# A graph network of four layers on one core: the fourth edge stage without a loop on the engines

## The reference, cut to what matters

```python
x_dst = tfn_features[edge_dst]                  # gathered, one row of 64 for each edge
wk = relu(edge_features @ k_w1 + k_b1) @ k_w2 + k_b2
wv = relu(edge_features @ v_w1 + v_b1) @ v_w2 + v_b2
k = tensor_product(x_dst, edge_sh, wk, Cqk)     # w * sum over 9 harmonics of sh_s * (x @ C_s)
v = tensor_product(x_dst, edge_sh, wv, Cv)
attn = einsum('ehd,ehd->eh', q[edge_src], k)    # 8 heads of 16
ex = exp(attn - segment_max(attn)[edge_src])
alpha = ex / (segment_sum(ex)[edge_src] + 1e-16)
upd = segment_sum(v * alpha, edge_src) @ W_out
out = tfn_features @ W_self + upd               # then a batch norm over the nodes
```

## Time and profile before

| | |
|---|---|
| Median of 3 runs | 3519.25 us (3516.62 to 3521.51) |
| The profiled execution's own time | 3510.65 us |
| Its span, first to last instruction | 3508.9 us |
| Fourth edge stage in it, first product to last addition | about 2151 to 3445 us |
| Mean granted TensorE clock over the span | 0.805 |

### The profile page before, as it was taken

The page is one execution under the profiler, slowest core; times in us unless marked ns, Lnnn a source line. Parts: engine busy times, 40 slices in busy tenths (PEclk is TensorE's granted clock), DMA queues, the critical chain, the costliest instruction groups (busy, mean ns, idle before and its releaser), DMA issues. The chain is left out here.

```text
span 3508.9 us, 58176 instructions
## 1 busy us (share of the span) xinstructions
PE 2551.3 (73%) x14132; PEld 2166.8 (62%) x14132; DVE 2280.8 (65%) x5044; ACT 1062.1 (30%) x2723; POOL 1789.0 (51%) x1813
## 2 busy tenths in 40 slices
PE   3778777514554444357777765999999999999986
PEld 2778776413443333245555544888888888888872
DVE  3555555337887887855556542677777777777775
ACT  1111111134554564111111101344444344443441
POOL 2777776066666663157777723444444344443400
PEclk7776777556555666589999967999999999999985
DMA  2443443265554552035445517988888888888830
GB/s 64 93 87 84 87 87 64 46 161 131 132 123 125 132 124 72 2 110 157 153 153 161 158 63 177 203 204 197 197 201 199 200 198 190 193 200 198 195 92 9
DMA packets 433884, 475.50 MB, mean 136 GB/s; under 512 B 200837, under 2 KB 304648, under 8 KB 433712
## 3 DMA queue, kind: packets, MB, share of 16 engines
q1 hardware_dynamic: 358832, 295.60, 35.9%
q0 software_dynamic: 59904, 123.64, 15.2%
q10 hardware_dynamic: 14976, 54.53, 4.5%
HBM read 408.18 MB, written 65.34 MB: 135 GB/s over the span
## 5 line engine op out<-in xcount | busy, mean ns | idle before, releaser
L1960 PE MATMUL psum<-ckv,z 128*128 128x256 f32 x4160 | 969.7, 384 | 0.0
L1960 PEld LDWEIGHTS psum<-ckv,z 128*128 128x128 f32 x4160 | 767.9, 191 | 98.5
L1823 POOL DMA_INDIRECT ga<-XX,src_i x416 | 398.1, 957 | 449.7 <-PE psum L1941 307.0
L985 POOL DMA_INDIRECT ga<-T,src_i x416 | 431.4, 1037 | 302.3 <-issue 112.5
L275 POOL DMA_INDIRECT ga<-T,src_i x416 | 401.3, 965 | 151.7 <-issue 124.4
L275 POOL DMA_INDIRECT ga<-TA,src_i x416 | 412.4, 991 | 126.7 <-issue 126.7
L2009 DVE TENSOR_TENSOR z<-psum,shb 128x2560 f32<-128x2560 f32 x104 | 293.7, 2824 | 125.8 <-PE psum L1941 78.5
L455 PE MATMUL psum<-wre,re 128*128 128x68 f32 x832 | 213.4, 349 | 142.1 <-DVE oneT L331 82.6
L1816 POOL TENSOR_TENSOR acc<-acc,wkv 128x512 f32<-128x512 f32 x104 | 114.3, 1099 | 332.7 <-DMA wkv<-WKV 316.4
L455 PEld LDWEIGHTS psum<-wre,re 128*128 128x128 f32 x832 | 173.4, 258 | 162.9 <-issue 153.9
L2050 DVE TENSOR_TENSOR acc<-acc,psum 128x256 f32 x416 | 175.4, 422 | 120.2 <-PE psum L1932 90.9
(11 more groups left out here) (349 smaller groups left out, 4862.8 us busy)
## 6 DMA issues: line engine op xcount, KB each, us to landing
shb<-in_ea SPq DMA_DIRECT2D x104, 640.0 KB
WKV<-wkvo ACTq DMA_DIRECT2D x104, 512.0 KB
shb<-in_ea SPq DMA_DIRECT2D x104, 512.0 KB
wkv<-WKV SPq DMA_DIRECT2D x104, 512.0 KB
dl<-DL SPq DMA_DIRECT2D x312, 128.0 KB, 3.5
acc<-QW SPq DMA_DIRECT2D x416, 64.0 KB
win<-TB SPq DMA_DIRECT2D x416, 32.0 KB
ga<-T,src_i POOLq DMA_INDIRECT x832
```

Source lines behind the costliest of these rows:

```text
L985: pool.indirect_dma_start(ga[:, ring(g) + t, :], None, T1, bass.IndirectOffsetOnAxis(ap=src_i[:, g * GT + t:g * GT + t + 1], axis=0)).then ...
L1823: pool.indirect_dma_start(ga[:, (g % GR) * GT + t, :], None, XX, bass.IndirectOffsetOnAxis(ap=src_i[:, g * GT + t:g * GT + t + 1], axis=0) ...
L1960: last = pe.matmul(kv_of(k)[:, t, :], z[:, k % 2, j, t * 128:(t + 1) * 128], ckv[:, j, :], start=(j == 0), stop=(j == NZ - 1))
```

## The change

In `each_step` the loop is written out: all fourteen passes of `body` stand one after another in the stream of PE, DVE, ACT and SP. In SP's functions four increments of the semaphore `e3_sp`, each between a wait and what follows, are dropped; nobody waits for that semaphore.

```diff
         def each_step(eng, body):
 
-            each_group(eng, body)
-            for k in range(UG):
-                body(NI, k)
+            for i in range(NI + 1):
+                for k in range(UG):
+                    body(i, k)
...
                     wait(sp, e3_wq, g - 1)
-                    sp.sem_inc(e3_sp, 1)
                     wait(sp, e3_ev, (g - 1) * 2)
-                    sp.sem_inc(e3_sp, 1)
                     sp.dma_start(wkv[:, k % 2].rearrange("p t f -> p (t f)"),
...
                         wait(sp, e3_oT, g - 1)
-                        sp.sem_inc(e3_sp, 1)
                         sp.dma_start(dl[:, k % 2, :], DL[:, cols].partition_broadcast(128)).then_inc(e3_dl[k % 2], 16)
                         wait(sp, e3_z, g - 1)
-                        sp.sem_inc(e3_sp, 1)
```

## The result

The changed kernel takes **3464.38 us** (median of 4 runs, 3462.65 to 3471.49), the kernel before, timed beside it, 3517.93 us (3509.20 to 3521.51). The medians differ by 53.5 us, where 35.8 were forecast. The ratio is 0.9855, with a 95% interval of 0.9832 to 0.9878, which stands for 51 us (43 to 59). The profiled execution of after is one of 3463.91 us (span 3462.2), so its distance to that of before (span 3508.9) is 46.7 us.

A forecast was written before the change was run, and what follows sets the result against it. PE was taken to bound the fourth edge stage, stalled by DVE's jump back. Terms of 28.1 + 3.1 + 4.6 = 35.8 us off the median of 3519.25 gave 3483.5 us, range 3472 to 3502 us.

The forecast's parts named there:

- The bound and the cause: Fourth edge stage: PE bounds it, and its eleven stalls before the sums come from DVE's jump back.
- First term: PE's idle time before the sums at eleven pass boundaries of the fourth edge stage goes: 28.1 us.
- Second term: Lost matmul overlap and slower restart after each PE stall: 0.28 us each, 3.1 us for eleven.
- Third term: PE's clock drops after two of the eleven stalls go: 4.6 us, bounds 0 and 25 us.
- The step from the profile to the median: Whole kernel: 35.8 us, read from the profiled execution, subtracted from a median 8.6 us above it.
- Streaming: Fourth edge stage: instructions streamed instead of reused, about 55 more packets, costing PE 0.
- the third rival: PE waits for its own streamed code: 3538 us at 1 us a packet, up to 3643 us; chance 0.06.
- Register work and increments: Address and wait-value instructions on four engines and SP's four semaphore increments go: value 0.
- The pause moves: Rival: DVE pauses 2.9 us elsewhere once in each pass; 3507 us, or 3495 if every second pass; chance 0.09.
- No change: Rival: the gap comes from the head of a pass and stays; gain 0.7 us, 3518.5 us; chance 0.05.
- Margin at the boundary: Pass boundary without the gap: DVE's first half of additions ends 0.25 us before PE arrives.
- Passes of 92.7 us: Sign in the changed profile: fourth-stage passes take 92.7 us throughout, 92.95 less the 0.28.

The follow-up runs named there:

- before_again: The kernel before, unchanged, profiled a second time in the first group; 3523.01 us, one run.
- dve_alone_loops: The changed kernel with DVE alone put back into its loop in the fourth edge stage; 3521.05 us, 1.0030 of the kernel before.
- before_third: The kernel before, unchanged, profiled a third time, on another chip; 3843.38 us, one run.
- dve_alone_straight: The kernel before with DVE alone written out in the fourth edge stage, the other engines looping; 3470.45 us, 0.9877 of the kernel before.
- the hinted loop: The kernel before with an instruction at the head of DVE's loop that announces the jump back; 3478.81 us, 0.9896 of the kernel before.
- all_stages_again: Repeat of the changed kernel with the loops of edge stages 1 and 3 written out too; 3761.18 us, 0.9711 of the kernel before.

## Why the prediction was right in place and short in size

**The bound and the cause** were right. PE had no idle time but those eleven stalls, they came from DVE's jump and from nothing else on the other engines, and they are gone.

**First term, PE's idle time, 28.1 us:** right for the profiled execution. The window says 25.4 for ten stalls and 0 after. Other executions with the same eleven stalls have 31.0 (before_again), 32.9 (dve_alone_loops) and 37.2 us (before_third), so it was at the low end.

**Second term, restarts, 0.28 us each:** fits. Restarts and clock together were put at 2.8 + 4.6 = 7.4 us for ten stalls, and the extra busy time is 7.0. For the profiled execution of before the sum was thus 32.8 us in ten passes, and the measured difference is 32.4: the sum is right for the execution that it was read from.

**Third term, the clock, 4.6 us:** this is the step that failed. The prediction took "all 4.6 us" because that was "the only one measured", and let the low end move by "four more drops of the clock", 8.6 us. That execution had the smallest loss of all those seen: in ten passes the clock took 4.2 us in it, and 9.5, 15.6 and 21.0 in three others (before_again, dve_alone_loops, before_third). In the others the drops followed on more of the stalls, and with stalls that were somewhat longer a jump cost 4.0 us (before_again, 40.2 / 10), 4.9 (dve_alone_loops) and 5.7 (before_third), where the sum had 3.3. Eleven jumps at 4.0 to 4.9 us are 44 to 54 us; dve_alone_straight measures 43 us (interval 35 to 52) for DVE's jumps alone, the changed kernel 51 (43 to 59). The clock is the larger part of what was missed: of the 7.8 us by which the ten jumps cost more in before_again than in the profile of before, 5.3 are the clock's and the rest idle time, and of the 16.4 in dve_alone_loops 11.4. The upper bound of 25 us for this term was worked out and stood in the text, and then wasn't used for the range, although both ends of an unknown cost belong in it: 28.1 + 3.1 + 25 = 56 us, a low end of 3463 us, would have held the result, by 1 us.

**The step from the profile to the median.** The prediction saw that ordinary executions of before are 8.6 us above the profiled one, and subtracted a loss that was read from the profiled one. The excess was most likely in part a larger loss: in before_again, an execution of 3523.01 us, the stretch from first to last `z` is 9.1 us longer than in the profiled one. That wasn't shown for the median runs themselves, which have no profile.

**Scatter outside the jumps.** The 5.6 us ahead of the stage and some 6 at the start of pass 1 are not the change's work by any row or run here; they are in the profiled pair, and how much of such is in the medians (51 us against 43 for DVE alone, with intervals that overlap) can't be told. So the prediction's mechanism is right, its third term too small, and for a part of the 17.7 us that it fell short the cause stays open.

**Streaming, 0:** right, with 47 packets of PE's for 55 forecast; the third rival, PE waiting for its own code, has no row at all. That PE is "the one engine that keeps the loop's code" was wrong: ACT and SP keep theirs too, and DVE's fetches were in a queue that the rows of before leave out. **Register work and increments, 0:** right. **The pause moves:** it didn't; there is no DVE wait for issue before `z` in after. **No change:** refuted by the gap's going; the branch with its test is worth 0.3 us a turn, by the hinted loop. Its argument that the same load stands at step 4 is right (a load of base addresses stands in each of the eight steps), though rows 9 don't show it. The 108 ns of the Trainium skill, "Advanced Engine Details and Errata", section Control Flow Timing, price only that part: the branch was 62 ns in the row, and the fetch behind it, 2.8 us and more, is what the change removed.

**Margin at the boundary, 0.25 us:** too small. DVE was 1.20 us ahead at the boundary shown, and a pause of 0.7 us was absorbed. Without the gap `z` starts 1.43 us behind PE's transposes at step 0, against 2.19 at step 4. It made no difference, and it errs on the safe side.

**Passes of 92.7 us:** 927.1 / 10 = 92.71.

## What to carry to other kernels

Read a hardware loop's price as the time between its taken branch and the first instruction of the next turn, engine by engine. Where it is microseconds, the loop's start is being fetched again at each jump: write the loop out, shorten it, or announce the jump, which here gives most of the gain (36 of 43 us) for one instruction a turn. And when short idles of a busy TensorE are removed, count the clock that falls behind some of them as a range over executions, not as the figure of one profile: here it took 4 to 21 us behind ten stalls at the same places.

## What was not expected of the hardware

- DVE loses 2.8 to 4.2 us at each jump over 397 instructions in the first group, and up to 4.8 in before_third; 0.3 us at 161 or 195 instructions; 2.9 to 3.2 at 401, in another stage.
- Placing the loop's head at the start of a block doesn't shorten the gap: 3.9 to 5.5 us in the one profile taken.
- Fetches for the looping DVE code are in the trace (56 packets of 8 KB in 1005 us, twice as many as the straight code takes), and with the jump announced they are nearly gone (4).
- Idle times of 2.1 to 4.1 us on an otherwise fully busy PE let the granted clock fall to 1.2 GHz behind some of them and not others, in the same kernel at the same places.
- On some executions single register instructions of SP take 0.7 to 1.3 us (2.1 in all_stages_again) instead of 0.03, and a stage whose loads SP issues becomes 29% longer (686.4 against 532.7 us).
